# Output products one head at a time over the next group, each fourth head turned by the DMA, key pages in two halves

## The reference, cut to what matters

```python
B, S, HID = 32, 32, 512          # sequences, tokens of each, width
D, HQ, HK = 128, 32, 8           # head width, query heads, key heads
q, k, v = x @ Wq.T, x @ Wk.T, x @ Wv.T          # 32, 8 and 8 heads
q, k = rope(rmsnorm(q) * q_norm_w), rope(rmsnorm(k) * k_norm_w)
kc, vc = k_cache[block_table], v_cache[block_table]   # 16 pages of 32 keys
k_all, v_all = concat(kc, k), concat(vc, v)     # 512 old keys + 32 new ones
scores = q @ k_all.T * SCALE     # masked by cache_seqlens
o = softmax(scores) @ v_all
return x + o.reshape(B, S, HQ * D) @ Wo.T
```

## Time and profile before

| | us |
|---|---|
| runs | 1046.19, 1046.97, 1050.0 (median 1046.97) |
| profiled execution | 1046.1, span 1044.3 |
| phase 2, first scores to last matmul | about 347 to 1041 |

### The profile page before, as it was taken

The page is one execution under the profiler, slowest core; times in us unless marked ns, Lnnn a source line. Parts: engine busy times, 40 slices in busy tenths (PEclk is TensorE's granted clock), DMA queues, the critical chain, the costliest instruction groups (busy, mean ns, idle before and its releaser), DMA issues.

```text
span 1044.3 us, 24950 instructions
## 1 busy us (share of the span) xinstructions
PE 982.7 (94%) x8329; PEld 779.9 (75%) x8329; DVE 795.1 (76%) x1705; ACT 717.4 (69%) x1959; POOL 493.7 (47%) x642
## 2 busy tenths in 40 slices
PE   4889999999889999899999999998999999999998
PEld 2678888887678788769768857965976986895793
DVE  6779999999997788758847856865784885786680
ACT  4898999988765778747746746754774774675670
POOL 5445665566881266516415523622441641552340
PEclk9999999999999999999999999999999999999999
DMA  5789999989989899778998998999899999899740
GB/s 202 247 278 336 322 390 367 385 279 398 380 288 326 309 337 343 266 192 294 323 235 267 357 234 243 328 241 228 301 291 243 294 329 241 260 354 249 240 148 11
DMA packets 268016, 296.49 MB, mean 284 GB/s; under 512 B 94064, under 2 KB 225648, under 8 KB 265328
## 3 DMA queue, kind: packets, MB, share of 16 engines
q1 hardware_dynamic: 249200, 227.65, 71.3%
q0 software_dynamic: 18688, 67.25, 19.3%
HBM read 231.77 MB, written 46.27 MB: 266 GB/s over the span
## 4 chain that ended last, share of the span: by engine, by line
PE 54%; DVE 16%; SPq 8%; DMA 7%; issue 6%; ACT 5%; POOL 2%; ACTq 0%; DVEq 0%; POOLq 0%
PE ps_o L1411 16%; PE ps_proj L1411 15%; PE ps_o L1489 8%; SPq L640 5%; PE ps_s L1449 4%; PE ps_s L1453 4%; PE ps_t L1460 3%; DVE probs L1154 2%; DMA vs<-v_pages,v_row 2%; DMA kt<-k_pages_t 2%; PE ps_rt L1559 2%; DVE rot L1282 2%; DVE c_stage L1310 2%; PE ps_o L1503 1%; ACT probs L930 1%
## 5 line engine op out<-in xcount | busy, mean ns | idle before, releaser
L865 POOL TENSOR_SCALAR probs<-probs,recip 128x544 f32<-128x544 f32 (+1 forms) x256 | 157.5, 615 | 382.2 <-DVE recip L1162 377.7
L930 ACT ACTIVATE probs<-probs,neg_max 128x544 f32<-128x544 f32 x256 | 191.3, 747 | 155.5 <-DVE neg_max L1154 154.7
L1154 DVE CUSTOM_DVE_ANT_0 probs<-ps_s,mask,row_scale 128x544 f32<-128x544 f32 x256 | 200.1, 782 | 126.3 <-PE ps_s L1453 123.5
L1489 PE MATMUL ps_o<-pt,vs 128*128 128x128 f16 x3072 | 214.3, 220 | 8.2 <-DMA pt<-wo 3.8
L1489 PEld LDWEIGHTS ps_o<-pt,vs 128*128 128x128 f16 x3072 | 192.3, 98 | 19.0 <-issue 6.6
L821 POOL TENSOR_TENSOR roped<-rot 128x256 f32<-128x256 f32 x160 | 144.2, 922 | 82.2 <-DVE rot L1274 76.3
L1411 PE MATMUL ps_proj<-wt_hi,x0t_hi 128*128 128x512 f32 x384 | 159.7, 416 | 8.0 <-DVE x0t_lo L1112 7.0
L1411 PE MATMUL ps_o<-wo,ot_hi 128*128 128x512 f16 x512 | 153.7, 382 | 10.4 <-DVE ot_lo L1186 10.4
L1411 PE MATMUL ps_proj<-wt_hi,x0t_lo 128*128 128x512 f32 x384 | 151.7, 395 | 0.0
L1411 PE MATMUL ps_proj<-wt_lo,x0t_hi 128*128 128x512 f32 x384 | 150.8, 393 | 0.0
L853 POOL DMA_INDIRECT vs<-v_pages,v_row x128 | 131.4, 1026 | 22.3 <-issue 20.2
(11 more groups left out here) (146 smaller groups left out, 1599.0 us busy)
## 6 DMA issues: line engine op xcount, KB each, us to landing
kt<-k_pages_t SPq DMA_DIRECT2D x512, 128.0 KB
c_nat<-in_L_cond_k_cache SPq DMA_DIRECT2D x32, 512.0 KB, 5.8
q_t<-stage SPq DMA_DIRECT2D x64, 256.0 KB, 7.3
c_nat<-in_L_cond_v_cache SPq DMA_DIRECT2D x32, 512.0 KB, 7.2
qt<-q_t SPq DMA_DIRECT2D x32, 512.0 KB, 6.2
w_nat<-in_L_cond_Wq SPq DMA_DIRECT2D x8, 1024.0 KB, 8.9
k_pages_t<-c_stage SPq DMA_DIRECT2D x16, 512.0 KB, 5.8
c_nat<-in_L_cond_Wo SPq DMA_DIRECT2D x16, 512.0 KB, 7.7
```

The source lines that it names most:

```text
L865: pool.tensor_scalar(part, part, col(recip, i), 1.0, ALU.mult, ALU.mult).then_inc(p_norm, 1)
L930: act.activation(pr, pr, ACT.Exp, bias=col(neg_max, i), scale=-1.0, accum_out=col(row_sum, i)).then_inc(a_exp, 1)
L1154: dve.tensor_tensor_reduce(out=probs_of(i), in0=ps_s[:, score_cols(i):score_cols(i) + KEYS], in1=mask[(i // HK) % 2][:, mask_at(i):mask_at ...
L1489: ins = pe.matmul(ps_o[n % 2][:, jl * P:(jl + 1) * P], v[:, part, :], pt[i % NPT][:, NCH * half + c, :], start=jl == 0 and c == 0 and k == ...
```

## The change

- **Output products.** The products of group g no longer fill 8 steps with 4 heads each. They stand one head a step at the end of nearly all steps of the next group (`Y_AT`: from the last step of the group itself to r = 28, two heads at r = 3 and 4). They have a PSUM bank of their own, `ps_y`; for it the banks for transposes go from 3 to 2 from step 28 on (`T_THIRD`). The last group's stand at the four last steps (4, 6, 6 and 16 heads).
- **Layout of the context.** `ot_hi` and `ot_lo` are stored so that a quarter of the tile comes free when a quarter of the heads has been multiplied. The 128 tokens of a head then lie 32 elements apart (groups 1, 3, 5, 7) or 8 apart (groups 0, 2, 4, 6), and the rows of residual and output of the even groups are in another order.
- **New values.** `vn` holds 3 x 32 rows (high, high, low) in place of 4 x 32 with zeros, and `ptn` the matching rows (high, low, high): 4 matmuls a half in place of 8. ACT and DVE each need two instructions of 32 partitions in place of one of 64, and POOL copies the high rows once more (`tn_copy`, L915 of the new file) in the step after.
- **Heads on the DMA.** Each step r mod 4 = 3 from step 52 on: 51 heads, evenly spread.
- **SP's order.** For each sequence b: the transpose of head 8b+7, queries and 8 pages for b+2, the transpose of head 8b+11, the other 8 pages, new values.
- **Output weights.** The last 20 heads are converted two in each five steps, up to step 48, in place of one in each two steps and then one a step, up to step 35.

```diff
-    TN, TNE, OE = HPC - 1, HPC, HPC + 2
-    DMA_FIRST, DMA_LAST, STAGED = 2, 11, 3
+    TN, TNE, TNC, OE = HPC - 1, HPC - 1, HPC, HPC + 2
+    DMA_FIRST, STAGED, T_THIRD = 52, 3, 28
 
     def by_dma(i):
-        g, r = divmod(i, GSTEPS)
-        return 0 < i < NP2 and g >= 1 and (DMA_FIRST if g > 1 else 8) <= r <= DMA_LAST
+        return DMA_FIRST <= i < NP2 and i % HPC == HPC - 1
...
+    t_banks = [0]
+    for kind, i in tjobs[1:]:
+        t_banks.append((t_banks[-1] + 1) % (3 if (i if kind == "t" else HPC * i + TN) < T_THIRD else NTB))
+    Y_AT = {r: (r + 1,) for r in range(-1, 3)} | {3: (4, 5), 4: (6, 7)} | {r: (r + 3,) for r in range(5, HQ - 3)}
+    Y_LAST = {-1: range(0, 4), 0: range(4, 10), 1: range(10, 16), 2: range(16, HQ)}
+    Y_OUT, Y_OUT_LAST = HQ - 3, 3
...
     def late_head(i):
-        if i >= LATE_PAIRS:
-            n = WO_EARLY + LATE_PAIRS // 2 + i - LATE_PAIRS
-        else:
-            n = WO_EARLY + i // 2 if i % 2 == 1 else HQ
-        return n if 0 <= i and n < HQ else None
+        k, r = divmod(i, 5)
+        n = WO_EARLY + 2 * k + r // 2
+        return n if i >= 0 and r in (1, 3) and n < HQ else None
...
-            PAGES_IN = {5: 0, 6: 4, 7: 8, 0: 12}
-            for i in range(NP2):
-                if by_dma(i + 2):
-                    turn_rows(i + 2)
...
+            BETWEEN = 8
+            for b in range(B):
+                turn_last(HK * b + HK - 1)
+                if b + 2 < B:
+                    load_queries(b + 2)
+                    load_pages(b + 2, 0, BETWEEN)
+                turn_last(HK * (b + 1) + HPC - 1)
+                if b + 2 < B:
+                    load_pages(b + 2, BETWEEN, NPP - BETWEEN)
+                    load_new_v(b + 2)
...
+            def tn_copy(n, normed):
+                pool.wait_ge(a_tnhi, n + 1)
+                pool.wait_ge(p_norm, normed)
+                pool.tensor_copy(ptn[n % 2][2 * SEQ:3 * SEQ], ptn[n % 2][0:SEQ]).then_inc(p_tncopy, 1)
+                pool.wait_ge(p_tncopy, n + 1)
...
+                for jl in range(HPC):
+                    m, e = divmod(jl, 2)
+                    ins = pe.matmul(ps_o[n % 2][:, jl * P:(jl + 1) * P], vn[b % 2][:, HPC * h + jl, :],
+                                    ptn[n % 2][:, e, m, :], start=False, stop=jl == HPC - 1, skip_group_check=True)
...
-                if y_part(i) is not None:
-                    project_out(*y_part(i))
+                for n in y_heads(i):
+                    project_out(y_group(i), n)
```

More of the change, by code:

```diff
@@ L117, in build @@
     key_pos = sb("key_pos", [P, MASK_W])
-    vn = [sb(f"vn{i}", [4 * SEQ, HK // 2, 2, 2 * D], F16) for i in range(2)]
+    vn = [sb(f"vn{i}", [3 * SEQ, HK, D], F16) for i in range(2)]
     phase1 = ExitStack()
@@ L213, in build @@
     pt = [sb(f"pt{i}", [P, 2 * NCH, P], F16) for i in range(NPT)]
-    ptn = [sb(f"ptn{i}", [4 * SEQ, 2, P], F16) for i in range(2)]
-    ot_hi = sb("ot_hi", [P, HQ, GB, SEQ], F16)
-    ot_lo = sb("ot_lo", [P, HQ, GB, SEQ], F16)
+    ptn = [sb(f"ptn{i}", [3 * SEQ, 2, 2, P], F16) for i in range(2)]
+    QUARTER = HQ // GB
+    ot_hi = sb("ot_hi", [P, HQ * GB * SEQ], F16)
+    ot_lo = sb("ot_lo", [P, HQ * GB * SEQ], F16)
     result = [sb(f"result{i}", [P, HID]) for i in range(2)]
     ps_s = psum("ps_s", [P, 3 * CH])
-    NTB = 3
+    NTB = 2
     ps_t = [psum(f"ps_t{i}", [P, CH]) for i in range(NTB)]
     ps_o = [psum(f"ps_o{i}", [P, HPC * P]) for i in range(2)]
+    ps_y = psum("ps_y", [P, HID])
     phase2.close()
@@ L781, in _ @@
         def _(pool):
-            for i in range(2):
-                pool.memset(vn[i][:], 0.0).then_inc(p_zero, 1)
             pool.memset(minus_one[:], -1.0).then_inc(p_zero, 1)
@@ L959, in ot_hi_of @@
                     all_stored(act)
-                g, first = divmod(n, NBG)
-                if first < NHALF and g >= 1:
-                    act.wait_ge(t_y, NHALF * (g - 1) + first + 1)
-                act.activation(ot_of(ot_hi, n), ps_o[n % 2][:].rearrange("p (h t) -> p h t", t=SEQ), ACT.Copy,
-                               scale=1.0 / P_SCALE).then_inc(a_othi, 1)
+                g, a = divmod(n // NHALF, GB)
+                if g >= 1:
+                    act.wait_ge(t_y, GB * (g - 1) + a + 1)
+                act.activation(ot_of(ot_hi, n), context(n), ACT.Copy, scale=1.0 / P_SCALE).then_inc(a_othi, 1)
             def wo_high(n):
@@ L1478, in weigh @@
                     pe.wait_ge(v_otlo, n - 1)
-                    g, first = divmod(n, NBG)
-                    if g >= 1 and 1 <= first <= NHALF:
-                        pe.wait_ge(v_res, NHALF * (g - 1) + first)
                 if by_dma(i):
@@ L1506, in weigh_new, with project_out @@
                 ins.then_inc(t_pvn, 1)
[L1508 removed]
+            def project_out(g, n):
+                h = head_at(g, n)
                 if g == 0:
[L1510 to L1519 removed]
+                    wo_done(pe, h + 1)
+                if n == 0:
+                    if g == 0:
+                        evacuated(pe, max(m for m in range(len(tjobs)) if t_banks[m] == NTB))
+                    else:
+                        pe.wait_ge(v_res, g)
+                    pe.wait_ge(v_otlo, NBG * (g + 1) - 1)
+                if n == HQ // NHALF:
+                    pe.wait_ge(v_otlo, NBG * (g + 1))
+                hi, lo = head_tokens(ot_hi, g, n), head_tokens(ot_lo, g, n)
+                ins = products(ps_y[:], [(hi, wo[:, h, 0, :]), (hi, wo[:, h, 1, :]), (lo, wo[:, h, 0, :])],
+                               first=n == 0, last=n == HQ - 1)
+                if n % QUARTER == QUARTER - 1:
```

169 lines of the change are left out of this document (80 added, 89 removed).

## The result

| | us |
|---|---|
| before, 4 runs beside the changed kernel | median 1046.58 (1039.41 to 1050.0) |
| after, 4 runs | median 1189.39 (1187.72 to 1190.77) |
| after / before | 1.138, 95% interval 1.135 to 1.142 |
| profiled execution of after | 1187.72, span 1185.9 |

The changed kernel is 13.8% slower. The forecast of 1036 lies on the wrong side, and the measured time is far beyond the upper end of its range (1012 to 1066).

The account below looks back on a forecast made before the run. The prediction took PE, working 94% of the span, to set the pace from group 1 on. From 1046.1 us, terms of -27.7 and +18 for key pages gave 1036 us, 1.0% faster, range 1012 to 1066.

Parts of the forecast that it names:

- the key pages: PE's new wait for a sequence's second eight pages at step 8b+13: +18 us, between 0 and 93.
- so I stand near the lower end: 2.7, a wait of 1.0: Last key page lands 2.7 us after issue, against 1.7 of play, so PE waits 1.0 us in 18 sequences.
- The bound from above, 5.9 us: Upper bound on a key page's landing, from 16 pages in a row that met the gathers: 4.2 us of wait.
- With the first gather of values at their end: Claim that pages come in eights with only the first gather at their end, used for the 2.7 us landing.
- the rival with late pages: Key pages issued late, behind gathers, land late: slower; at a landing of 4.0 us, +47, 1065 us. Chance 0.20.
- The point of decision: At 1.5 us of wait for key pages, a landing of 3.2, the change is no longer faster.
- In 6 of them ... no wait: In 6 of 24 sequences, 6 heads of products in steps r = 1 to 4 give 1.3 us more play: no wait.
- New values, -14.2: 4 matmuls a half fewer on PE, 0.22 us in 64 halves: -14.2 us; added rows lie beside PE.
- Output products, -22.1: Waits at the output products' edges go, 18.0 us, and PE's late resumption after 27 waits, 4.1: -22.1 us.
- The rival with the strided stationary operand: Output products get slower as a head's tokens lie 64 or 16 bytes apart: 135 us, 1171 us. Chance 0.05.
- Two banks, +10.5: Transposes wait for two banks, 1.7 us a half in 5 halves of group 1, about 2 in group 0: +10.5 us.
- Heads on the DMA, +5.7: 51 heads go over the DMA in place of 64, so 13 more transposes at 0.44 us: +5.7 us.

Follow-up runs that it names:

- experiment 7: Changed kernel without the gathers of values from the third sequence on, weighing the first two sequences' values again: 1054.27 us in one run.
- experiment 5: Kernel before with only the new values' part of the change (3 x 32 rows, 4 matmuls a half, POOL's copy): 1051.87 us, ratio 1.010.
- experiment 1: Changed kernel with 16 pages of a sequence ahead of its second DMA transpose instead of 8: 1095.19 us; with 12 ahead: 1079.26 us.
- experiment 4: Changed kernel with 8 pages before the transpose of head 8b+7, 8 after it: 1088.16 us; also turned probabilities first on ACT and DVE, steps 28 to 51: 1077.41 us.
- experiment 8: Second kernel of experiment 4 with a sequence's four gathers issued in pairs in two steps instead of one in each of four: 1061.46 us, ratio 1.017.
- experiment 9: Second kernel of experiment 4 with one head in eight on the DMA, heads-first also behind step 51: 1041.62 us; then low half first on DVE: 1027.94 us.

## Why the prediction was wrong, point by point

It was wrong above all in one term of the sum, the key pages, and in what that term left out. The predicted span was 1036.4 - 1.8 = 1034.6 (what lies around the span is 1.8 us); measured it is 1185.9, 151.3 more.

**The step that failed: "so I stand near the lower end: 2.7, a wait of 1.0".** The place, the count and the play were right. In the chain PE starts step 8b+9 at 669.06; the eighth page was forecast 8.55 later, at 677.61, and was issued at 677.59. PE was to want it 10.28 after the start, at 679.34, and its wait begins there (684.16 - 4.82). That is a play of 1.75 us, forecast 1.7; over the 24 it is 1.55 in the mean. What failed is the landing: 6.52 us here and 6.0 in the mean, in place of 2.7. The bound from above, 5.9 us, was about the mean. I set it aside since "those pages stood behind twelve others", and took the one stretch where the traffic stopped, four pages without a gather, as what eight pages with gathers would look like. It was a good forecast of the wrong case: without gathers the last page takes 2.6 us in the mean (experiment 7). "With the first gather of values at their end" was wrong too: by the timeline of POOL all four fall between the first page and the landing of the last. Their times could have been laid beside the pages' on PE's clock in the same way as everything else was. Experiment 7 gives this its size: without gathers the term is 26.4 us, with them 108.3.

**The second thing left out: the clock.** The forecast had read from the earlier trace rows that a wait of 3.8 us leaves the clock at 0.51, and took half of 6 us off for that one wait; it put nothing beside its own new waits, in the rival with late pages neither. It is 51.9 us behind the 24 waits, 2.2 each. In that rival, at 2.3 us a wait, this would have weighed about as much as the wait itself where the clock fell.

Together: 160.2 in place of 18 is 142.2 of the 151.3 us.

**The point of decision was right, the chance was not.** The rival "the pages land late" said that from 1.5 us of wait on the change is slower. That is what happened, at 4.5 us. It had 0.20 for its chance and stopped at a landing of 4.0.

**"In 6 of them ... no wait".** The play of 1.3 us more in every fourth sequence is there: their six waits are 3.6 us in the mean (4.12, 3.99, 1.97, 3.91, 3.65, 4.20), the other eighteen 4.8. It was not enough to clear them.

**New values, -14.2: right in this kernel, not by itself.** A half has 4 matmuls and 0.23 us (697.34 to 697.57), as forecast. Put into the kernel before alone it loses 1.0% (experiment 5), since "beside PE" holds only where DVE has room. That the spread output products make this room is argued from where those waits stand; no run has the two alone.

**Output products, -22.1: right by the rows, though no run has them alone.** None of the waits for `ot_lo` and the residual is left, those for the maximum are down from 6.5 to 2.0 us, and a head costs 0.65 us as before. The rival with the strided stationary operand falls: the three matmuls of a head take 690.84 - 690.18 = 0.66 us, against 0.64 to 0.65 before.

```profile
690.18 0.61 PE L1450 MATMUL ps_y<-wo,ot_hi 128*128 128x512 f16 x2
...
690.84 0.38 PE L1507 MATMUL ps_t<-fixed,probs 128*64 128x128 f32 x2
```

The loads did get slower, though. Tile `ot_hi`, weight loads of the changed kernel (ns, least, median, most):

```profile
L1450 PEld LDWEIGHTS ps_y<-wo,ot_hi x512: 136/146/168, 432.1 to 1181.9; 128*128 128x128 f16 x171
```

Before, the median was 98 ns, and the loads of `vs` in `weigh`, whose layout is unchanged, stay at 98. The Trainium skill ("SBUF — State Buffer", section on the DMA port swizzle) has a penalty for each access that crosses to a new 16-byte line, and the trace agrees in kind, at a step of 16 as of 64 bytes. It costs no time, since the matmul beside the load takes 216 ns: the argument of the forecast, that up to twice the time of a load is hidden, held.

**Two banks, +10.5: right in place, too low in size.** Forecast were waits of 0.47 and 1.2 us in five halves of group 1; the timeline has, in four of them,

```profile
442.96 0.38 PE L1507 MATMUL ps_t<-fixed,probs 128*64 128x128 f32 x2 [0.47 <-DVE pt L1219]
...
459.76 0.63 PE L1499 MATMUL ps_t<-fixed,probs 128*128 128x128 f32 x4 [1.32 <-DVE pt L1219]
```

In all it is 15.6 us (11.2 + 4.4), 5.1 more. The 2.3 us at the end of group 0 were forecast ("about 2"). What was not is a sixth half, the first of group 1, with 1.12 and 1.32, and 2.6 us outside these places: 1.6 in three waits in group 0 and 0.9 in one at 1159. Behind the wait of 2.3 us the clock was at 0.51 for 2 us, another 1.6 us (experiment 7, 418.96 to 422.36 where full clock takes 1.81).

**Heads on the DMA, +5.7.** The count of matmuls is as forecast. The "8 us of play" of a transpose were enough in the changed kernel itself, where none was late; in every order with two heads a sequence that brought all the pages forward, the transpose of head 8b+7 came late, and with all sixteen pages ahead that of 8b+11 too (experiments 1, 4 and 8). None of the orders tried had room for two heads and sixteen pages a sequence beside the gathers; that none can is not shown.

**What is left.** Without its gathers the kernel has a span of 1052.5, 17.9 above the forecast: 8.4 of it the waits for pages, 5.1 those for the banks, 3.3 the low clock behind two waits for pages and 1.6 that behind a wait for a bank. That is 18.4. In the changed kernel 142.2, 5.1 and 1.6 leave 2.4 of the 151.3 us. The forecast took off 4.1 us since PE resumes 0.15 us late after each of 27 waits, and added nothing of the kind behind the 41 new ones; that this is the rest is argued, not shown. A slip besides: the lower end of its range, the pages in time with half the banks' wait, is 1013 us by its own numbers, not 1012.

**The Trainium skill's figure** ("DMA: Bandwidth & Descriptors", section on latency) of about 2 us of fixed cost a DMA, more when loaded, would have made the term +5, by the forecast's estimate. The last page of a sequence took 6.0 us in the mean here, and 2.6 without the gathers: the trace agrees with the "more", three times the figure.

## What to carry to other kernels

Before you put a transfer close to its deadline, lay every transfer that can travel in that stretch on one clock, those of the other queues too, and take its landing from a row with the same load; the landing on empty engines is no middle value. A wait on a DMA that is long enough to drop PE's clock has to be priced with what the clock takes after it, here 2.2 us on top of 4.5. And where one engine has only a few tenths of a microsecond to spare in a step, the order of its instructions (which one frees the buffer that is awaited?) can be worth more than what the change was to win: here 14 us for the order of a few instructions on DVE and ACT.

## What the runs showed of the hardware

- The last key page of a sequence (128 KB) took 4.9 to 7.3 us from issue to landing, 6.0 in the mean of 24, with gathers and a transpose beside it, and 2.0 to 3.8, 2.6 in the mean of 21, at the same place with no gathers (experiment 7). A transpose behind eight pages took 8.19 (experiment 4).
- POOL's gathers move 67.25 MB in 18688 packets, 3.6 KB each, everything else on SP's queue 224.23 MB in 243152, 0.92 KB each:

```profile
q1 hardware_dynamic: 243152, 224.23, 60.9%
q0 software_dynamic: 18688, 67.25, 17.0%
```

  Whether the larger packets are why pages lose so much to gathers was not tried.
- The clock was at 0.50 for 4 us behind a wait of 4.82 us and for 2 us behind one of 2.74. Behind waits of 1.97 (changed kernel, at 759.05) and 2.20 us (experiment 7, at 1001.40) it first stayed at full speed and fell to 0.50 about 1 us later, with PE at work; behind one of 2.14 (experiment 7) it did not fall. The length of the wait alone does not tell it.
- Reading PSUM and writing SBUF in the new layout of `ot_hi` and `ot_lo` cost nothing that the trace shows: 580 ns in the median on ACT against 577, 670 on DVE against 672. Loading the stationary operand with a step of 16 or 64 bytes between columns took 146 ns against 98, hidden beside a matmul of 216.
- Two instructions of 32 partitions x 256 elements on DVE took 0.42 us each, as long as the one of 64 partitions that they replace.
- PE paid 0.50 us for a wait that the profile lists as 0.31 (experiment 9, 28 halves).
